# Second quantisation of the last stage: both steps of every tile from VectorE to GpSimd

## The reference

```python
def rmsnorm(x):
    return x * jax.lax.rsqrt(jnp.mean(x * x, axis=-1, keepdims=True) + EPS)
def act_quant(x):
    scale = 127.0 / jnp.clip(jnp.max(jnp.abs(x), axis=-1, keepdims=True), 1e-05)
    q = jnp.clip(jnp.round(x * scale), -128.0, 127.0) / scale
    return x + jax.lax.stop_gradient(q - x)
def bitlinear(x, w, b):
    xq = act_quant(rmsnorm(x))
    wq = weight_quant(w)
    return jnp.einsum('bsd,fd->bsf', xq, wq) + b
...
h = bitlinear(x, w1, b1)            # 128 -> 512 features
h = jax.nn.gelu(h, approximate=False)
return bitlinear(h, w2, b2)         # 512 -> 128 features
```

## Time and profile before

| | us |
|---|---|
| median of three runs | 622.02 |
| the profiled execution | 623.42 |
| its span on the core | 621.7 |
| busy: TensorE / VectorE / ScalarE / GpSimd | 507.4 / 448.4 / 262.8 / 137.9 |
| feed stage, about | the last 48 us, with its first tiles beside the cross attention |
| second quantisation, first L1715 to last L1718 | 599.04 to 617.33 |

### The profile page before, as it was taken

How to read it: one execution, slowest core, us unless ns; L and a number is a source line. 1 busy time by engine, 2 the same in 40 slices (tenths; PEclk the granted TensorE clock), 3 DMA queues, 4 the chain that set the end, 5 groups by cost and what they waited for, 6 DMA issues and landing times.

```text
span 621.7 us, 8890 instructions
## 1 busy us (share of the span) xinstructions
PE 507.4 (82%) x3146; PEld 291.8 (47%) x3146; DVE 448.4 (72%) x1162; ACT 262.8 (42%) x452; POOL 137.9 (22%) x102
## 2 busy tenths in 40 slices
PE   3997899999999999999998435565774999999533
PEld 1344666665566666666665101122222655555212
DVE  6599666765783566765464589999954778889785
ACT  5531355655542234333242355555401354444552
POOL 8533000000000000400000058999950100000100
PEclk9999799998999999999999756887776899999855
DMA  5000160000100000000000000000001000000001
GB/s 129 25 13 1 55 184 2 1 2 2 44 1 0 1 1 14 22 6 1 0 1 1 1 0 0 0 0 1 2 0 43 1 2 1 2 3 1 2 4 30
DMA packets 10767, 9.25 MB, mean 15 GB/s; under 512 B 2050, under 2 KB 9540, under 8 KB 10724
## 3 DMA queue, kind: packets, MB, share of 16 engines
q1 hardware_dynamic: 10724, 8.69, 5.0%
HBM read 6.98 MB, written 0.52 MB: 12 GB/s over the span
## 4 chain that ended last, share of the span: by engine, by line
PE 63%; DVE 29%; ACT 3%; issue 3%; POOL 1%; DVEq 0%; POOLq 0%; ACTq 0%
PE PS L1117 18%; PE PS L696 9%; PE PS L1143 9%; DVE VA L1605 6%; DVE PS L1592 6%; PE PS L759 5%; DVE PS L1598 3%; PE PS L683 3%; PE PS L744 3%; PE PS L735 3%; PE PS L716 2%; PE PS L450 1%; PE PS L769 1%; PE PS L428 1%; DVE E L557 1%
## 5 line engine op out<-in xcount | busy, mean ns | idle before, releaser
L1117 PE MATMUL PS<-XNT,KSA 128*128 128x512 f32 x256 | 118.0, 595 | 0.0
L906 ACT ACTIVATE E<-PS 128x512 f32<-128x512 f32 x128 | 71.2, 596 | 67.2 <-PE PS L744 41.0
L1131 DVE TENSOR_TENSOR E<-E,PS 128x512 f32<-128x512 f32 x64 | 43.9, 687 | 55.9 <-ACT E L1125 55.5
L1125 ACT ACTIVATE E<-PS 128x512 f32<-128x512 f32 x64 | 38.1, 597 | 104.1 <-PE PS L1117 103.8
L744 PE MATMUL PS<-QM,KP 32*128 32x256 f32 x512 | 81.3, 399 | 0.8 <-ACT E L906 0.8
L696 PE MATMUL PS<-KP,QP 32*128 32x256 f32 x512 | 78.0, 405 | 2.1 <-ACT QP L883 1.7
L1143 PEld LDWEIGHTS PS<-KSA,E 128*128 128x128 f32 x512 | 62.1, 192 | 16.3 <-issue 15.0
L1117 PEld LDWEIGHTS PS<-XNT,KSA 128*128 128x128 f32 x256 | 45.3, 191 | 40.4 <-issue 40.2
L1143 PE MATMUL PS<-KSA,E 128*128 128x128 f32 x512 | 62.4, 275 | 1.3 <-DVE XN L1345 1.3
L287 PE MATMUL PS<-KSA,select 128*128 128x512 bf16 x64 | 26.1, 500 | 44.7 <-ACT KSA L1483 37.7
L961 DVE CUSTOM_DVE_ANT_0 SCR<-PS,KSA 128x256 f32<-128x256 f32 x128 | 46.5, 420 | 22.0 <-PE PS L696 20.9
(11 more groups left out here) (267 smaller groups left out, 822.7 us busy)
## 6 DMA issues: line engine op xcount, KB each, us to landing
KSA<-in_w SPq DMA_DIRECT2D x2, 1024.0 KB, 6.7
X<-in_x SPq DMA_DIRECT2D x2, 256.0 KB, 3.4
SCR<-in_ctxT SPq DMA_DIRECT2D x1, 512.0 KB, 5.5
KP<-OT SPq DMA_DIRECT2D x16, 32.0 KB
SCR<-in_fside SPq DMA_DIRECT2D x1, 512.0 KB, 4.8
KP<-QM SPq DMA_DIRECT2D x16, 32.0 KB
out_x<-X SPq DMA_DIRECT2D x8, 64.0 KB, 1.5
wx<-in_w_x SPq DMA_DIRECT2D x1, 384.0 KB, 6.7
```

Source lines behind the costliest of these rows:

```text
L906: act.activation(slot(m, j), weight_bank(m, j), ACT.Exp).then_inc(sig("exps"), 1)
L1117: ins = pe.matmul(bank(2 * (g % 3) + o), w[:, e, c * P:(c + 1) * P], XNT[:, tokens_of(p)], start=True, stop=True)
L1125: act.activation(E6[:, 4 + g % 2, :], bank(2 * (g % 3)), ACT.Silu).then_inc(sig("silu"), 1)
L1131: dve.tensor_tensor(E6[:, g % 4, :], E6[:, 4 + g % 2, :], bank(2 * (g % 3) + 1), ALU.mult)\
```

## The change

`quant_factors` can raise a named semaphore with its last instruction in place of a link; `second_factors` uses it, with the name `second_factors`. `requantise` goes from VectorE's list to GpSimd's: for each tile GpSimd waits for the factors of its half, does step one, waits for its own result, waits for the transposes of tile j-2 and does step two. The four tiles of the first half stand in GpSimd's list ahead of the third power, `power(2)`; the four of the second half behind it. In VectorE's list the calls of `requantise` are gone, `finish(2)` is behind `mean_square(1)`, and `finish(4)` to `finish(7)` follow the second factors directly.

```diff
-        def quant_factors(dve, ch, w, s):
+        def quant_factors(dve, ch, w, s, signal=None):
...
-            ch.link(dve.scalar_tensor_tensor(fac[:, s], fac[:, s], 127.0, rstd[:, s], ALU.mult, ALU.mult))
+            ins = dve.scalar_tensor_tensor(fac[:, s], fac[:, s], 127.0, rstd[:, s], ALU.mult, ALU.mult)
+            if signal is None:
+                ch.link(ins)
+            else:
+                ins.then_inc(sig(signal), 1)
...
-                quant_factors(dve, ch, 1, s)
-
-            def requantise(j):
-                ch.link(dve.tensor_scalar(HB[:, j, :], GG[:, j, :], fac[:, j:j + 1], ROUND, ALU.mult, ALU.add))
-                if j >= 2:
-                    dve.wait_ge(sig("g_turned"), j - 1)
-                dve.tensor_scalar(GQ[:, j % 2, :], HB[:, j, :], -ROUND, 127.0, ALU.add, ALU.min)\
-                    .then_inc(sig("q2"), 1)
+                quant_factors(dve, ch, 1, s, "second_factors")
...
             second_factors(0)
-            requantise(0)
             feed_hidden(dve, 5)
             feed_peak(dve, 4)
-            requantise(1)
             feed_hidden(dve, 6)
             feed_peak(dve, 5)
             finish(0)
-            requantise(2)
             feed_hidden(dve, 7)
             feed_peak(dve, 6)
             finish(1)
-            requantise(3)
-            finish(2)
             feed_peak(dve, 7)
             mean_square(1)
+            finish(2)
             finish(3)
             second_factors(1)
-            requantise(4)
-            requantise(5)
-            for j in (6, 7):
-                finish(j - 2)
-                requantise(j)
-            finish(6)
-            finish(7)
+            for j in range(4, NT):
+                finish(j)
...
             power(1, tiles_of(0), "feed_square", 1)
+
+            def requantise(j):
+                pool.wait_ge(sig("second_factors"), j // 4 + 1)
+                pool.tensor_scalar(HB[:, j, :], GG[:, j, :], fac[:, j:j + 1], ROUND, ALU.mult, ALU.add)\
+                    .then_inc(sig("rounded"), 1)
+                pool.wait_ge(sig("rounded"), j + 1)
+                if j >= 2:
+                    pool.wait_ge(sig("g_turned"), j - 1)
+                pool.tensor_scalar(GQ[:, j % 2, :], HB[:, j, :], -ROUND, 127.0, ALU.add, ALU.min).then_inc(sig("q2"), 1)
+
+            for j in range(4):
+                requantise(j)
             power(2, tiles_of(1), "feed_square", 2)
+            for j in range(4, NT):
+                requantise(j)
```

## The result

The changed kernel takes 630.27 us (median of four, 629.85 to 631.43) against 622.01 us; the ratio is 1.0131, interval 1.010 to 1.0162. The forecast was 621.3 us in a range of 619.7 to 627.2, so the result lies 3.1 us above the range; a rise of over 1% had been given a chance of 0.06. The profiled execution took 631.43 us against 623.42, its span 629.7 against 621.7: 8.0 us more in both.

A forecast was written before the change was run, and what follows sets the result against it. VectorE's full queue was taken to bound the first half, a serial chain of waits the second. First half -0.52 and second -0.21 gave -0.73 us, so 622.02 became 621.3 us, range 619.7 to 627.2.

The forecast's parts named there:

- Step two has its exact row: L1964, 0.62 us: Step two of the quantisation on GpSimd: priced at 0.62 us from an existing GpSimd instruction, with no range.
- Step one, a = 0.89 from 0.62 to 1.90: Step one's time on GpSimd, estimated as L1963's 0.62 us plus half of L390's 0.55 excess; ends 0.62 and 1.90.
- rival 3: Step one on GpSimd: the operand from memory is free, 0.62 us, giving 619.9 us; chance 0.17.
- The sums: Both halves of the last stage: change of 5a - 5.18 us, or 8a - 8.84 from a = 1.22 on; a is step one's time.
- ScalarE's period in the first half: First half, ScalarE full from gelu to gelu: 1.39 us of work plus 0.49 to the next gelu, 1.88.
- a - 1.41: First half: shift of the start of the last factors, -0.52 us; a is step one's time on GpSimd.
- 4a - 3.77: Second half: four tiles from the factors take 4a + 2.76 against 6.53 us, change -0.21; a is step one's time.
- Rival 1, GpSimd paces both halves: Last stage: step one pays per column, so GpSimd sets the pace; +4.9 us at 1.72, +6.4 at 1.90; chance 0.25.
- ScalarE idle between gelus: First half: named sign that the forecast is wrong, meaning GpSimd paces; the forecast had ScalarE full there.
- The queue on GpSimd: GpSimd's list: `power(2)` stands behind `requantise(3)`, fourth tile done at 605.33, last copy starting at 607.0: no cost.
- Rival 2, mutual holding: Last stage: VectorE and GpSimd hold each other up, +0.8 us, 622.9 us; chance 0.08.
- The second half's wait behind `finish`: Second half: 6.53 us for 3.64 of own work, as L1718 of tiles 6 and 7 queue behind a `finish` awaiting TensorE.

The follow-up runs named there:

- e1: Kernel before the change, plus 20 forms of elementwise instructions on GpSimd in its idle stretch after 54 us, results unused; 622.15 us in one run against 621.42.
- e2: Changed kernel with step two's two operations turned, min first and then add, same values; ratio to the kernel before 1.0104.
- e3: Changed kernel with step two as times 1, then minus 12582912, clip at 127 left out; ratio to the kernel before 0.9981.
- e4: Changed kernel with step one alone on GpSimd, step two back on VectorE at new places in its list; ratio to the kernel before 0.9958.
- e5: Kernel before, nothing on GpSimd, VectorE's second-half list turned: requantise 4 to 7, then finish 4 to 7; ratio to the kernel before 0.9950.

## Why the prediction was wrong

- **"Step two has its exact row: L1964, 0.62 us"**: this step failed. Put right, it alone turns the forecast into 629.1 us (622.02 + 7.1; the sum is below). L1964 has the engine, the shape and both types of step two, but multiplies and adds; step two adds and takes a minimum. That was called exact without comparing the operations. The doubt about operations that the prediction raised for L390, the dear row, it did not raise for the cheap one. Measured 1.92 (e1, e2), and 0.62 as soon as the pair is multiply and add (e3). No bound was set around it, so the range left it out.
- **Step one, a = 0.89 from 0.62 to 1.90**: 0.69 measured, below the 0.75 to 1.2 that the forecast counted as its own and near rival 3's 0.62. The half excess was too careful in its place; L390 was slow for being a comparison alone, which the prediction had named as possible (e1).
- **The sums**: near, and right in their build. Put the excess of step two, 1.30, on top of a: 8 x (0.69 + 1.30) - 8.84 = +7.1; e2 has +7.32, the changed kernel +7.98. At a = 0.70 and 1.38 they gave -1.7 and +2.2 against -1.96 and +2.43. What was mis-sized is ScalarE's period in the first half: 1.88 was taken, e3 has 1.75 to 1.76. With it the first half came 1.05 shorter in e3 where a - 1.41 gave 0.71; the second half, 0.91 shorter against the 0.97 of 4a - 3.77, fits. The changed kernel's further 0.66 over e2 stand in its starts: GpSimd's next instruction began 0.10 after step two's end (599.92 + 1.94 to 601.96), in e2 0.02 before it. Why two pairs of the same length differ in this stays open.
- **Rival 1, GpSimd paces both halves**: this is what happened, with its consequences (gelus 2.79 apart, copy of tile 3 behind the fourth tile, the whole stage bound by GpSimd), but through step two and beyond its far end. The prediction had its mechanism at 0.25 and hung it on the wrong instruction. Its own sign of being wrong came true, ScalarE idle between gelus: the copy at 610.92 found it idle for 0.92.
- **The queue on GpSimd**: `power(2)` did stand behind `requantise(3)`, but that ended at 610.23 and L1708, which it needs as well, at 610.25. Behind L1708 alone it starts 0.08 later (e3 too), and so it did: no cost, even with the slow step two, though by a margin of nearly nothing.
- **Rival 2, mutual holding**: not in the changed kernel, where step one has its 0.69 as in e1 and VectorE's hidden layer and peak keep their 0.75 and 0.69. It appears in e4, with a VectorE step two in the way: 0.96 to 1.11, 0.85 on average. The forms named as free of it, with one input in PSUM, stayed free.
- **The second half's wait behind `finish`**: read rightly. Turning the list takes it away with no second engine and brings 2.98 us (e5), where the move with a fast pair in both halves brought 1.96 (e3).

## What to carry to other kernels

A row prices an instruction only if its operations agree too, not just engine, shape and types; on GpSimd two such rows can be a factor of three apart. Before moving work to a second engine, ask whether the old engine was short of time or merely had the work in a bad place in its list: here turning the list gave 2.98 us, and the second engine, for the one step that is cheap there and with the list fitted to it, at most 1.3 more. If an operation that isn't needed or can be split makes a pair slow, take it out or make two fast instructions of it.

## What the runs showed of the hardware

- GpSimd's two-operation form with constants over 512 f32 columns took 0.61 to 0.66 us for multiply-add, add-multiply and min-max, and 1.92 to 1.95 for add-min, min-add, multiply-min, min-multiply, add-add and add-max (e1). For add-min, 1.06 at 256 columns and 1.95 at 512 is 3.4 ns per column (estimate, from two points); multiply-add went from 0.40 at 256 to 0.62 at 512, about 0.8 ns per column, an estimate with the reserve that the row of 256 reads int32.
- A single operation of this form on GpSimd took 1.49 us, more than twice a fast pair, while a plain copy to bf16 took 0.61 (e1). Adding a multiplication by 1 to a lone addition made it faster: 1.49 (L1988) against 0.62 (L1980).
- A number per partition from memory cost 0.07 us (e1).
- Step one on GpSimd took 0.69 us beside VectorE's hidden layers (one input in PSUM) and peaks (a reduction), and 0.96 or 1.11 where it met VectorE's step two, a one-input instruction in SBUF; once VectorE's step two was the one held, 0.91 instead of 0.43 (e4).
